# Edge counting in a graph network: ScalarE makes 4 of 8 source one-hots, and packed counts are taken apart in another way

## The reference, cut to what matters

```python
edge_index = jnp.stack([src, dst])                    # 20000 edges
agg = jax.ops.segment_sum(x[src], dst, num_segments=625)
h = (1.0 + eps) * x + agg                             # layer 0, eps = 0
```

## Time and profile before

| | us |
|---|---|
| median of 3 runs | 1226.74 (1226.6 to 1229.4) |
| the profiled execution's own time | 1228.88 |
| its span in the profile | 1227.1 |
| PE busy | 1103.0 (90%) |
| DVE busy | 841.5 (69%) |
| ACT busy | 509.6 (42%) |
| POOL busy | 718.8 (59%) |

### The profile page before, as it was taken

How to read it: one execution, slowest core, us unless ns; L and a number is a source line. 1 busy time by engine, 2 the same in 40 slices (tenths; PEclk the granted TensorE clock), 3 DMA queues, 4 the chain that set the end, 5 groups by cost and what they waited for, 6 DMA issues and landing times. The chain is left out here.

```text
span 1227.1 us, 20866 instructions
## 1 busy us (share of the span) xinstructions
PE 1103.0 (90%) x6814; PEld 1011.1 (82%) x6814; DVE 841.5 (69%) x1631; ACT 509.6 (42%) x897; POOL 718.8 (59%) x972
## 2 busy tenths in 40 slices
PE   7889788859999999999999999988799999997775
PEld 6778777739998799888998899876799889996664
DVE  7999878565665756756676656754478857876645
ACT  5334333323542145322551235323476636765311
POOL 3452490363557755576656765596556857577662
PEclk9889988769999999999999999998899999998888
DMA  5000010231202112023021211222201110020101
GB/s 118 1 1 1 1 32 35 87 102 52 78 2 72 51 54 78 1 79 96 2 77 44 78 45 70 87 94 70 83 1 51 55 35 1 21 84 14 63 27 42
DMA packets 40264, 60.79 MB, mean 50 GB/s; under 512 B 13864, under 2 KB 14114, under 8 KB 39537
## 3 DMA queue, kind: packets, MB, share of 16 engines
q1 hardware_dynamic: 40162, 59.47, 15.1%
HBM read 52.76 MB, written 5.41 MB: 47 GB/s over the span
## 5 line engine op out<-in xcount | busy, mean ns | idle before, releaser
L353 POOL TENSOR_TENSOR w_lo<-w_raw,w_hi 128x512 fp32r<-128x512 f32 x152 | 201.7, 1327 | 12.7
L313 PE MATMUL ps<-yt_hi,w_hi 128*128 128x314 f32 x640 | 201.9, 315 | 4.4 <-DVE yt_lo L1955 3.0
L313 PE MATMUL ps<-yt_hi,w_lo 128*128 128x314 f32 x640 | 198.0, 309 | 0.0
L313 PE MATMUL ps<-yt_lo,w_hi 128*128 128x314 f32 x640 | 197.7, 309 | 0.0
L432 POOL TENSOR_SCALAR prob<-prob,rinv 125x628 f32<-125x628 f32 x160 | 126.9, 795 | 105.3 <-DVE rinv L417 86.5
L376 ACT ACTIVATE pt_hi<-ps 125x625 fp32r<-125x625 f32 x160 | 109.4, 695 | 111.1 <-PE ps L335 110.0
L661 PE MATMUL ps<-oh_s,oh_d 125*125 125x314 bf16 x800 | 126.5, 320 | 22.4 <-DVE oh_s L559 19.4
L661 PEld LDWEIGHTS ps<-oh_s,oh_d 125*125 125x125 bf16 x800 | 113.1, 147 | 35.5 <-DVE oh_s L559 28.1
L350 POOL TENSOR_SCALAR w_hi<-w_raw 128x512 fp32r<-128x512 f32 x152 | 98.8, 650 | 71.9 <-DMA w_raw<-L_gnn_wo 37.7
L313 PEld LDWEIGHTS ps<-yt_hi,w_hi 128*128 128x128 f32 x640 | 122.1, 191 | 6.9 <-DVE yt_lo L1955 3.6
L335 PE MATMUL ps<-ident,prob 125*125 125x125 f32 x800 | 110.5, 275 | 15.7 <-POOL prob L432 10.9
(11 more groups left out here) (288 smaller groups left out, 2876.8 us busy)
## 6 DMA issues: line engine op xcount, KB each, us to landing
w_raw<-L_gnn_m_w SPq DMA_DIRECT2D x8, 1024.0 KB, 5.4
w_raw<-L_gnn_W SPq DMA_DIRECT2D x6, 1024.0 KB, 5.4
w_raw<-L_gnn_wv SPq DMA_DIRECT2D x4, 1024.0 KB, 6.5
w_raw<-L_gnn_wq SPq DMA_DIRECT2D x4, 1024.0 KB, 5.4
w_raw<-L_gnn_wk SPq DMA_DIRECT2D x4, 1024.0 KB, 7.3
w_raw<-L_gnn_wo SPq DMA_DIRECT2D x4, 1024.0 KB, 6.1
w_raw<-L_gnn_Wv SPq DMA_DIRECT2D x2, 1024.0 KB, 6.2
w_raw<-L_gnn_Wq SPq DMA_DIRECT2D x2, 1024.0 KB, 5.3
```

Of the source, the lines that this page charges most:

```text
L313: ins = pe.matmul(out_ap, lhs(i, kk), rhs(j, kk), start=kk == 0 and n == 0, stop=kk == count - 1 and n == 2)
L353: pool.tensor_tensor(w[slot][1][:, kk, 0:cols], w_raw[slot][:, kk, 0:cols], w[slot][0][:, kk, 0:cols].bitcast(FP32), ALU.subtract).then_in ...
```

## The change

ACT makes the source one-hots of slots 1, 3, 5 and 7 (4 of 8). Packed counts are taken apart without `words`: ACT reads the bank, multiplies by 1/4096, subtracts 0.49 and lets the conversion to int32 round, which gives `above`; DVE then computes below = packed - 4096 * above in one scalar_tensor_tensor whose second input is the PSUM bank. `below` and the lower half of `cnt` are now FP32, the upper half stays int32. DVE does all five of these steps in a row after its tile t4 of the next chunk. PE's wait at the chunk's start is now for s_below (DVE's result) in place of s_words (ACT's). ACT moves between its 2nd and 3rd one-hot of the chunk. POOL starts with the `below` half, and waits for `above` after it.

```diff
-    OHA = (2, 5)
+    OHA = (1, 3, 5, 7)
...
-    words = sb("words", "pt", [R, TILES, H2], I32)
+    offset = sb("offset", "pt", [R, 1])
     above = sb("above", "ot", [R, TILES, H2], I32)
-    below = sb("below", "ot", [R, TILES, H2], I32, HALF)
+    below = sb("below", "ot", [R, TILES, H2], FP32, HALF)
...
+            steps.done(pool.memset(offset[:], -0.49))
...
-                    pool.wait_ge(s_above, n + 1)
                     if c < CHUNKS - 1:
                         pool.wait_ge(s_below, n + 1)
-                        pool.tensor_tensor(cnt_i[:, m, 0:H2], cnt_i[:, m, 0:H2], below[:, m, :],
+                        pool.tensor_tensor(cnt[:, m, 0:H2], cnt[:, m, 0:H2], below[:, m, :],
                                            ALU.add).then_inc(s_added, 1)
+                    pool.wait_ge(s_above, n + 1)
                     pool.tensor_tensor(cnt_i[:, m, H2:W], cnt_i[:, m, H2:W], above[:, m, :],
...
             def unpack(c, m):
-                dve.wait_ge(s_words, n + 1)
+                dve.wait_ge(s_above, n + 1)
                 if c > 0:
                     dve.wait_ge(s_added, 2 * (n - TILES) + 2)
-                dve.tensor_scalar(above[:, m, :], words[:, m, :], BITS, None,
-                                  ALU.logical_shift_right).then_inc(s_above, 1)
-                dve.tensor_scalar(below[:, m, :], words[:, m, :], (1 << BITS) - 1, None,
-                                  ALU.bitwise_and).then_inc(s_below, 1)
+                dve.scalar_tensor_tensor(out=below[:, m, :], in0=above[:, m, :], scalar=-PACK, in1=bank(n % 8),
+                                         op0=ALU.mult, op1=ALU.add).then_inc(s_below, 1)
             for c in range(CHUNKS):
                 for o in range(OH):
                     onehots(c * CT + o, o, c == 0)
+                    if c > 0 and o == TILES - 1:
+                        for m in range(TILES):
+                            unpack(c - 1, m)
...
-                    if c > 0 and o < TILES:
-                        unpack(c - 1, o)
...
-                        act.wait_ge(s_below, n - TILES + 1)
-                    act.activation(words[:, m, :], bank(n % 8), ACT.Copy).then_inc(s_words, 1)
+                        act.wait_ge(s_added, 2 * (n - TILES) + 2)
+                    act.activation(above[:, m, :], bank(n % 8), ACT.Identity, bias=offset[:, 0:1],
+                                   scale=1 / PACK).then_inc(s_above, 1)
...
-                onehots(c, 0, c == 0)
+                onehots(c, 0, c == 0, range(2))
                 if c > 0:
                     move(c - 1)
+                onehots(c, 0, c == 0, range(2, len(OHA)))
...
-                    pe.wait_ge(s_words, (c + 1) * TILES - 8)
+                    pe.wait_ge(s_below, (c + 1) * TILES - 8)
```

More of the change, by code:

```diff
@@ L48 @@
 PACK = float(1 << 12)
-BITS = 12
 class Jobs:
@@ L467, in build @@
     s_oh, s_oha, s_away, s_ohu = sem("onehots_ready"), sem("onehots_of_act_ready"), sem("distances"), sem("onehots_used")
-    s_cf, s_words = sem("counts_filled"), sem("counts_moved")
+    s_cf = sem("counts_filled")
     s_last, s_float = sem("last_counts_added"), sem("counts_as_floats")
@@ L510, in _ @@
             for m in range(TILES):
-                pool.tensor_copy(cnt_i[:, m, t_slice(m)], ident[0:R, 0:R]).then_inc(s_zero, 1)
+                first, last = m * R, (m + 1) * R
+                middle = min(max(first, H2), last)
+                if middle > first:
+                    pool.tensor_copy(cnt[:, m, first:middle], ident[0:R, 0:middle - first]).then_inc(s_zero, 1)
+                if middle < last:
+                    pool.tensor_copy(cnt_i[:, m, middle:last], ident[0:R, middle - first:R]).then_inc(s_zero, 1)
             def add(c):
@@ L516, in add @@
                     n = c * TILES + m
-                    before = (s_zero, TILES) if c == 0 else (s_added, 2 * (n - TILES) + 2)
+                    before = (s_zero, TILES + 1) if c == 0 else (s_added, 2 * (n - TILES) + 2)
                     pool.wait_ge(*before)
-                    pool.wait_ge(s_above, n + 1)
                     if c < CHUNKS - 1:
                         pool.wait_ge(s_below, n + 1)
-                        pool.tensor_tensor(cnt_i[:, m, 0:H2], cnt_i[:, m, 0:H2], below[:, m, :],
+                        pool.tensor_tensor(cnt[:, m, 0:H2], cnt[:, m, 0:H2], below[:, m, :],
                                            ALU.add).then_inc(s_added, 1)
+                    pool.wait_ge(s_above, n + 1)
                     pool.tensor_tensor(cnt_i[:, m, H2:W], cnt_i[:, m, H2:W], above[:, m, :],
@@ L596, in _ @@
                     dve.wait_ge(s_below, (CHUNKS - 1) * TILES + m)
-                    dve.tensor_tensor(cnt[:, m - 1, 0:H2], cnt_i[:, m - 1, 0:H2], below[:, m - 1, :],
+                    dve.tensor_tensor(cnt[:, m - 1, 0:H2], cnt[:, m - 1, 0:H2], below[:, m - 1, :],
                                       ALU.add).then_inc(s_float, 1)
@@ L609, in move, with onehots @@
                     if c > 0:
-                        act.wait_ge(s_below, n - TILES + 1)
-                    act.activation(words[:, m, :], bank(n % 8), ACT.Copy).then_inc(s_words, 1)
-            def onehots(c, j, first=False):
-                for n, o in enumerate(OHA):
+                        act.wait_ge(s_added, 2 * (n - TILES) + 2)
+                    act.activation(above[:, m, :], bank(n % 8), ACT.Identity, bias=offset[:, 0:1],
+                                   scale=1 / PACK).then_inc(s_above, 1)
+            def onehots(c, j, first=False, which=range(len(OHA))):
+                for n in which:
+                    o = OHA[n]
                     tile, nth = j * OH + (c * CT + o), j * len(OHA) + (c * (CT // OH) * len(OHA) + n)
```

## The result

The median is **1214.15 us** (5 runs, 1213.86 to 1218.62) against 1226.74 before; the ratio is 0.9898, 95% interval 0.9873 to 0.9923: faster by 12.6 us, with an interval from 9.4 to 15.6. The forecast was 1219.9 with a range from 1215.5, so the direction was right and the size was not: the gain is nearly twice the 6.85 us foretold.

The account below looks back on a forecast made before the run. DVE, held up by POOL, was taken to bound the counting stage. Terms +1.65 (chunk 0), -1.6, -2.0, -1.3, -2.2 (chunks 1 to 4), -1.4 (tail) sum to -6.85 us: 1226.74 to 1219.9, range 1215.5 to 1226.8.

Parts of the forecast that it names:

- What bounds the stage: Counting stage: DVE bounds it, held up by POOL's adds and weight splits; PE's loads idle 28.1 us for its one-hots.
- the terms of chunk 0, chunk 4 and the tail: Counting stage: chunk 0 loses 1.65 us to a wait for ACT, chunk 4 gains 2.2, the tail gains 1.4.
- chunk 3: Counting stage, fourth chunk: 24.9 us against 26.17, a gain of 1.3, with no fall of the clock.
- rival B: Unpack step dearer, at 0.81 us or queued behind POOL: gain only 3.6 us, 1223.1; chance 0.14.
- DVE gets one step through per POOL instruction: Beside POOL's adds and weight splits: one DVE step passes per POOL instruction; a pair of split steps takes 1.94 us.
- DVE gets 8 steps: Chunks 1 and 2, during POOL's weight splits: eight DVE steps pass in 7.75 us, to T = 17.5.
- PE falls to half clock here: Chunks 1 and 2, weight splits: PE at 1.31 us a tile until about T = 19; chunks gain 1.6 and 2.0.
- span 1227.1 to 1220.25: Whole kernel: the stage's terms sum to -6.85 us, passed on whole to the span.
- A: Clock also falls in chunks 3 and 4, costing 1.4 us each: gain 4.1, 1222.6; chance 0.22.
- C: ACT's one-hot pair in the loops slower than 1.13 us, up to 2.0: gain 2.9, 1223.8; chance 0.05.
- D: POOL's back-to-back adds keep DVE out for two instructions per step: slower by 6.7 us, 1233.4; chance 0.06.
- E: No gain arrives: later stages absorb it or chunk 0 loses more, about 1226.5 us; chance 0.08.

Follow-up runs that it names:

- ln_split: The changed kernel with ACT normalising three blocks of x in chunk 0 and two after chunk 1's second one-hot group; 1211.41 us, ratio 0.9872.
- before_late2: The kernel before the change with one idle DVE memset ahead of its first one-hot; 1226.54 us, ratio 1.0011.
- before_late4: The kernel before the change with two idle DVE memsets ahead of its first one-hot; 1229.28 us, ratio 1.0027.
- oha_only: The kernel before the change with ACT's one-hot slots 1, 3, 5, 7 in place of 2, 5, old unpacking kept; 1227.69 us, ratio 1.0001.
- pairs_1256: The changed kernel with ACT's one-hot slots 1, 2, 5, 6 in place of 1, 3, 5, 7; 1216.57 us, ratio 0.9922.

## Why the prediction was wrong in size

**Right.** What bounds the stage, and the terms of chunk 0, chunk 4 and the tail, each within 0.1 us; chunk 3 within 0.4. PE's new wait in chunk 0 was foretold as 1.9 us from 27.95 and is 1.87 ending at 29.89; ln_split shows that it is ACT's normalising that makes it. The new step is 476 ns on average and 461 to 483 over all 25, beside POOL's adds or not, so rival B falls. Here the Trainium skill can be weighed too ("VectorE: DVE Perf Modes", the TRN2 errata): worked out from its table, an estimate, this step takes 452 ns and the two removed 2 x 224, so no gain in the trade; the rows have 476 against 2 x 313, and the measurement decides. The same section of the Trainium skill says under its table that the row for SBUF comes out too low, which the 313 confirm and the forecast left out. The Trainium skill's page "GPSIMD Engine Reference" (Key points), which names contention only for DVE steps in a two-port mode or with two SBUF inputs, agrees with the 461 to 483.

**The step that failed first**: "DVE gets one step through per POOL instruction", used in chunks 1 and 2 as "DVE gets 8 steps", and with it "PE falls to half clock here". It held for the order of before. It depends on the order of steps: where an oh_s waited out the short w_hi, the oh_d behind it began 0.07 us ahead of w_lo and got through (47.20 against 47.27); where an oh_d waited it out, w_lo began first (46.85 against 46.87). With the new order (oh_s, oh_d, oh_d) it is three steps in 2.16 us in three of four pairs, and with (1, 2, 5, 6) back to two in three of four. DVE got 11 steps through in the 8.45 us of the splits (44.57 to 53.02), not 8 in 7.75. In chunk 1 the forecast had t16 done at T + 19.2 and 15 tiles to go; measured, t18 begins at T + 18.66 (53.53 us) with 14 to go. Of the 1.15 us, 0.65 is the tile that was to be counted at half clock (1.31 for 0.66) and 0.5 the quicker feed, by the forecast's own terms. Much the same in chunk 2. Together 2.4 of the 2.9 us by which the stage was missed. The bounds of the range had the clock (-1.4 each, more than the 0.65 that the sum has for it) but not the feed. In chunk 3, where the rule was used too, DVE's first oh_d began ahead of the third add and got through, and t10 came 0.5 us early: the other 0.4.

**The step that failed second**: the sum "span 1227.1 to 1220.25", which hands the stage's gain on whole and has no term and no width for the 1074 us behind the barrier. The stage as measured gives 1226.74 - 9.7 = 1217.0, inside the range; what takes the median to 1214.15 lies behind the barrier. PE's long waits there are nearly the same in both kernels. The stretches between them aren't of one length: from 152.9 us, before_late2 and before differ by 4.0 us with the stage before it equal. One part of after's 5.2 us goes with the clock: from 74 to 87 us behind the barrier before has half clock for 13.7 us, as before_late2 has, and after only from 78 to 85. At PE's 450th matmul behind the barrier (115 us) after is 1.8 us ahead of before, and before_late2 is level with it. Whether 2 to 3 us of the gain are owed to the change (a stage that starts elsewhere meets the clock's falls elsewhere, as before_late4 has it) or to scatter stays open; by median less barrier, before and its variants without the new unpacking have 1072.2 to 1073.8, those with it 1070.6 to 1073.3.

**Rivals.** A (the clock falls in chunks 3 and 4): it fell in neither. Its price was read too low: rows 11 give 3.4 us at half clock, not 2.9, so 1.7 us a chunk. C: ACT's pair in the loops took 1.3 us at PE's pace, waits for PE included; PE's waits for ACT's oh_s are 2.3 us in all, of which 1.87 in chunk 0. D (two POOL instructions per DVE step): the opposite came true. E: nothing was absorbed.

How much of chunks 1 and 2 is owed to the clock and how much to the feed isn't separated in full. In chunk 1 PE's matmuls were busy 27.0 us before and 23.5 after, but part of the 3.5 us lay in time in which PE would have waited for DVE. oha_only doesn't settle it: its clock stayed at 1.00 in chunk 1 and the chunk got no shorter, but it holds a new wait of PE, 2.46 us, for ACT's move. Its chunk 2 gained 1.8 us with the old unpacking. What is shown is that both parts of the change shorten chunk 2 (the slots by 1.8 or 2.1 us, the unpacking by 1.2 or 1.5, each without and with the other), and that one fall of 3.4 us costs some 1.7 (pairs_1256, chunk 1 against 2).

## What to carry to other kernels

When the steps of two engines hold each other up, don't count "one step per instruction" from one order of steps: read which of the long and the short steps meet in the trace, and work it out again for the new order. Where the bound engine is starved in bursts, try a greater lead (tiles made ahead of the burst) before removing work: placing the unpacking three tiles later gave 3.7 us in the stage for one changed constant. And give the untouched rest of a long kernel a width in the range, from two profiles of the same code if they are there.

## What the runs showed of the hardware that was not expected

- Beside POOL's weight splits two or three DVE steps came through per pair of POOL steps, by their order: 3 in 2.16 us where an oh_s stood behind the short w_hi, 2 in 1.94 where an oh_d did.
- ACT's move with a scale and an offset takes 524 ns where the plain copy took 0.43 us, and five in a row 2.18 us where it was 1.73.
- The granted clock stayed at 1.00 though PE was busy only 2.77 of the 4 us from 48 to 52; the forecast had taken half clock there.
- The same 1070 us of code behind the same start took 1070.2 and 1074.2 us in two profiles.
